# A two-layer graph network on one core: how the second layer contracts the scalars of x with the aggregate, and where its one-hots are made

## The chip, the cores and the metric

The kernel runs on one core of a Trainium2 chip. The metric is the device time of one execution in microseconds (us); before the change it is 6655.41 us, the median of three runs (6651.92 to 6660.94).

## The reference, cut to what matters

There are 12500 nodes with 160 features each (64 scalars, 32 vectors of three components) and 200000 edges. Two layers run one after the other; each builds a message per edge, sums the messages by destination node into an aggregate of the same form as x, and updates each node with bilinear products of x and the aggregate, before a layer norm.

```python
agg = segment_sum(msg, row)                 # 12500 x 160
a0, a1 = agg[:, :64], agg[:, 64:].reshape(n, 32, 3)
u0 = einsum('nu,nv,uvw->nw', xs, a0, Wu_ss) * INV64 \
   + einsum('nui,nvi,uvw->nw', xv, a1, Wu_vv) * (INV_SQRT3 * INV32)
u1 = einsum('nu,nvi,uvw->nwi', xs, a1, Wu_sv) * c + einsum('nui,nv,uvw->nwi', xv, a0, Wu_vs) * c
u0 = u0 + xs @ Lu_s * INV8
u1 = u1 + einsum('nui,uw->nwi', xv, Lu_v) * INV_SQRT32
x = layernorm(x + node_features + concat([u0, u1]))
```

The change is about the first term of `u0` in the second layer, the scalar product of xs (64) and a0 (64) with the 64x64x64 tensor `Wu_ss`.

## The kernel before, in words

The nodes are cut into NT = 100 tiles of HM = 125 nodes. The edges were sorted by an early stage into 2176 slots per tile (17 blocks of 128, padded), and the messages of a layer are written into those slots in DRAM. A layer's node sweep then goes over the tiles. In layer 1 (the second; layers are numbered 0 and 1 in the code) only this sweep runs, in `node_sweep`, which takes NT + 2 steps and is written out in full for every step. The five engines each have their own program of the sweep, `node_step`, and meet at semaphores only. In step t:

- SyncE (SP) issues the transfers: tile t of x (`xt`, L569, after the h of tile t - 2), the messages of tile t + 1 (`msgs`, L384) and its spilled sums once the edges of tile t - 1 are summed, and the output of tile t - 2 (L404, L405) when it is normed.
- TensorE (PE) does `bilinear(0)` to `bilinear(5)` of tile t - 1, `sum_edges` of tile t (L1368: 17 blocks of one-hot times messages into `node_ps`), the transposes of the vector products `turn_q`, `scalar_sums`, `turn_y`, `vector_products` and `linear`.
- VectorE (DVE) does `scalars(0..3)` (L1043), the mixed products (L1079, two of three components), their sums (`mixed_sum`, L1092) and `h` (L1122) of tile t - 1, in that order, and a reciprocal (L1127) of tile t - 2 between the two sums.
- ScalarE (ACT) copies the mixed products out of PSUM (`prods_out`, L1606), does the statistics of tile t - 2, the copies of x, of the aggregate and of the transposes, and at the end of the step the 17 squared distances (`distances`, L1714) and the selection (`selections`, L1720) that make the one-hots of tile t + 1 in the only buffer, `onehot`.
- GpSimd (POOL) does the third component of the mixed products of tile t - 1 (L763), and the outer products of vectors (`q3`, L737) with their two sums (L772) of tile t, once both `turn_q` of tile t - 1 have read `q3`.

The scalar product is made in two contractions. `bilinear(r)`, r = 0 to 3, multiplies the weights with the transposed aggregate (contraction over 64 on each half of the array) into a pair of PSUM banks of 1000 columns. DVE multiplies them with the transposed scalars of x into `zs` (L1043). `scalar_sums` adds them over 128 partitions with a band of ones, 32 matmuls of 32 output rows (L1325):

```python
for r in range(R0):
    for hh in range(2):
        o = BAND - row_sum(r, hh)
        for q in range(QUARTER):
            mm = te.matmul(to[32 * q:32 * q + 32, 0:HM], band[:, o:o + 32], zs[:, r, hh, q, :], ...
```

`bilinear(r)` for r of 2 and more waits until DVE has used the banks of r - 2. Layer 0 has the same products, between its own work for the edges of layer 1; it keeps them.

## Time and profile before

| what | value |
|---|---|
| median of three runs | 6655.41 us (6651.92 to 6660.94) |
| the profiled execution, its own time | 6649.59 us |
| its span in the profile | 6647.9 us |
| mean granted TensorE clock | 0.918 of full speed |
| busy: PE, DVE, ACT, POOL | 82%, 82%, 56%, 77% of the span |
| the sweep of layer 1 | from about 4850 us to the end |

The profile names each group of instructions by its source line, engine and the tensors it writes and reads ("out<-in"). "x" is the number of instructions, "busy" the time in which they ran. "Idle before" is time that the engine stood still ahead of them, with the instruction that released it. L1306 and L1307 are the matmuls of `bilinear(0..3)`, L1309 and L1310 those of `bilinear(4)` and `bilinear(5)`, L1336 those of `vector_products`. The timeline gives the start and the duration of merged pieces. A float32 matmul appears as two instructions.

### The profile page before, as it was taken

How to read it: one execution, taken by the hardware profiler on the slowest of the kernel's cores; microseconds unless marked ns; L12 is line 12 of the kernel's file. 1: busy time of each engine (PE TensorE's matmuls, PEld its weight loads, DVE VectorE, ACT ScalarE, POOL GpSimd, SP SyncE). 2: the span in 40 equal slices, each digit the busy share in tenths (PEclk: the TensorE clock that was granted, in tenths of full speed). 3: DMA queues.
4: the chain of work that ended last, by engine and by line, in shares of the span. 5: the costliest groups of instructions: out<-in, count | busy, mean ns of one | idle time of the engine just before them, and what ended most of it. 6: DMA issues, size and time to landing. Idle time of an engine off the chain costs nothing.

```text
span 6647.9 us, 144690 instructions
## 1 busy us (share of the span) xinstructions
PE 5431.9 (82%) x52095; PEld 4342.4 (65%) x52095; DVE 5458.2 (82%) x7292; ACT 3710.3 (56%) x11578; POOL 5133.5 (77%) x4006
## 2 busy tenths in 40 slices
PE   5566666666666499999999999999589999999998
PEld 3445444554545377777777777777467777777777
DVE  6777777777778589999999999989378888888988
ACT  2333333333333366666666666666267777777776
POOL 2777777777777568888888888877778888888887
PEclk7778888778788799999999999999799999999999
DMA  7888888888886278888888888888422232222222
GB/s 226 257 256 260 256 257 256 258 253 258 260 257 204 92 236 275 278 272 272 275 275 273 272 278 265 271 264 269 153 88 94 95 103 94 94 96 102 94 95 76
DMA packets 681145, 1380.94 MB, mean 208 GB/s; under 512 B 106047, under 2 KB 487661, under 8 KB 654447
## 3 DMA queue, kind: packets, MB, share of 16 engines
q1 hardware_dynamic: 527695, 1090.23, 52.2%
q0 software_dynamic: 152736, 281.45, 12.5%
q8 instruction: 416, 6.82, 0.4%
q14 instruction: 298, 2.44, 0.1%
HBM read 587.20 MB, written 784.08 MB: 206 GB/s over the span
## 4 chain that ended last, share of the span: by engine, by line
PE 36%; SPq 14%; DVE 13%; POOL 13%; DMA 9%; ACT 8%; issue 6%; POOLq 0%; DVEq 0%; ACTq 0%
PE node_ps L1368 11%; PE prods_ps L1306 6%; DMA rec<-edge_recs 5%; DVE upd L1092 5%; ACT onehot L1714 5%; POOL q L737 4%; PE prods_ps L1325 4%; SPq L353 4%; POOL q L772 3%; SPq L379 3%; PE s_ps L1222 3%; DMA table<-tab 2%; DVE zs L1043 2%; POOL picks_sb L763 2%; PE prods_ps L1309 2%
## 5 line engine op out<-in xcount | busy, mean ns | idle before, releaser
L654 POOL DMA_INDIRECT slots<-pay,slot_all x3136 | 3246.8, 1035 | 1037.0 <-issue 813.1
L1714 ACT ACTIVATE onehot<-node_iota,msgs 128x125 f32<-128x125 f32 x3400 | 1028.1, 390 | 121.9 <-POOLq L698 121.9
L1368 PEld LDWEIGHTS node_ps<-msgs,onehot 128*125 128x125 f32 x6800 | 932.0, 188 | 139.4 <-ACT onehot L1720 83.1
L1368 PE MATMUL node_ps<-msgs,onehot 128*125 128x160 f32 x6800 | 980.8, 303 | 35.9 <-ACT onehot L1720 25.3
L1092 DVE TENSOR_REDUCE upd<-work 125x48 f32<-125x3072 f32 x300 | 1004.1, 3347 | 6.8
L1079 DVE TENSOR_TENSOR work<-prods_ps,yv 125x1024 f32<-125x1024 f32 x800 | 931.3, 1217 | 52.0 <-PE prods_ps L1310 51.1
L737 POOL TENSOR_TENSOR q<-xt,yv 125x3072 f32<-125x3072 f32 x100 | 547.7, 5477 | 302.1 <-PE turn_ps L1355 285.1
L1500 ACT COPY picks_sb<-s_ps 125x512 f32<-125x512 f32 x392 | 229.9, 586 | 938.6 <-PE s_ps L1204 706.3
L1190 PE MATMUL prods_ps<-bucket_onehot,after_bf 128*128 128x500 bf16 x392 | 174.9, 446 | 667.5 <-DVE bucket_onehot L909 666.9
L1222 PE MATMUL m_ps<-win,picks_sb 125*128 125x160 f32 x3136 | 654.2, 336 | 68.6 <-ACT pay L1515 61.7
L1222 PEld LDWEIGHTS m_ps<-win,picks_sb 125*128 125x128 f32 x3136 | 519.4, 215 | 145.6 <-ACT pay L1515 91.2
L1190 PEld LDWEIGHTS prods_ps<-bucket_onehot,after_bf 128*128 128x128 bf16 x392 | 40.3, 103 | 715.4 <-DVE bucket_onehot L909 714.2
L1043 DVE TENSOR_TENSOR zs<-prods_ps,x_t 128x1000 f32<-128x1000 f32 x400 | 460.6, 1192 | 55.9 <-PE prods_ps L1307 55.9
L1306 PE MATMUL prods_ps<-spill_tab,w_bil 64*128 64x125 f32 x3200 | 439.9, 281 | 58.0 <-DVE zs L1043 58.0
L772 POOL TENSOR_TENSOR q<-q 125x1024 f32<-125x1024 f32 x200 | 473.0, 2365 | 15.7
L1043 DVE TENSOR_TENSOR zs<-prods_ps,spill_tab 128x1000 f32<-128x1000 f32 x400 | 460.4, 1192 | 10.9 <-PE prods_ps L1307 10.8
L1306 PE MATMUL prods_ps<-a_t,w_bil 64*128 64x125 f32 x3200 | 440.6, 281 | 29.9 <-DVE zs L1043 28.2
L1307 PE MATMUL prods_ps<-a_t,w_bil 64*128 64x125 f32 x3200 | 457.9, 285 | 0.0
L1307 PE MATMUL prods_ps<-spill_tab,w_bil 64*128 64x125 f32 x3200 | 457.3, 284 | 0.0
L1515 ACT COPY pay<-m_ps 128x320 f32<-128x320 f32 x784 | 331.0, 422 | 222.2 <-PE m_ps L1222 221.1
L1306 PEld LDWEIGHTS prods_ps<-spill_tab,w_bil 64*128 64x128 f32 x3200 | 385.7, 187 | 98.1 <-DVE zs L1043 76.1
L1720 ACT ACTIVATE onehot<-onehot,ones_f 128x1375 f32<-128x1375 f32 (+2 forms) x300 | 444.3, 1481 | 3.4
(268 smaller groups left out, 13339.8 us busy)
## 6 DMA issues: line engine op xcount, KB each, us to landing
msgs<-slots SPq DMA_DIRECT2D x200, 1428.0 KB, 6.4
slots<-zero SPq DMA_DIRECT2D x183, 1386.0 KB
win<-table SPq DMA_DIRECT2D x784, 160.0 KB
picks<-picks_sb SPq DMA_DIRECT2D x196, 512.0 KB
picks_sb<-picks SPq DMA_DIRECT2D x196, 512.0 KB
table<-tab SPq DMA_DIRECT2D x200, 350.0 KB
slots<-pay,slot_all POOLq DMA_INDIRECT x3136
spill_in<-spill_sums SPq DMA_DIRECT2D x200, 80.0 KB, 6.1
```

Of the source, the lines that this page charges most:

```text
L654: g.indirect_dma_start(out=slots[layer][:, :], out_offset=bass.IndirectOffsetOnAxis(ap=slot_all[:, j:j + 1], axis=0), in_=pay[q][:, j - UB ...
L737: g.tensor_tensor(q3[0:HM, VV * i0:].rearrange("p (i u v) -> p i u v", u=V, v=V), xt[nb][0:HM, S:D].rearrange("p (u i) -> p i u", i=3)[:, ...
L772: add = g.tensor_tensor(q3[0:HM, 0:VV], q3[0:HM, 0:VV], q3[0:HM, VV * (j + 1):VV * (j + 2)], ALU.add)
L1043: ve.tensor_tensor(zs[:, r, :, :, :], prods_ps[(nb + r) % 2][:, :].rearrange("p (h c) -> p h c", h=2)[:, :, 0:QUARTER * HM].rearrange("p h ...
L1079: ve.tensor_tensor(wk[:, i, :, :].rearrange("p w (h k) -> p h w k", h=2), prods_ps[(nb + r) % 2][0:HM, :].rearrange("p (h w k) -> p h w k" ...
L1092: ve.tensor_reduce(upd1[:, :, w0:w0 + ROUND // KV], mixed_part(r), AX_X, ALU.add).then_inc(s["upd"], 1)
L1222: mm = te.matmul(to[:, D * j:D * j + D], (pick_b[q] if layer else pick_n[hh])[0:WROWS, P * (2 * p + j):P * (2 * p + j) + P], win[q][0:WROW ...
L1306: te.matmul(to[:, HM * q:HM * q + HM], w.bil[0:S, o:o + P], a2_t[nb][0:S, :], start=True, stop=True)
L1307: mm = te.matmul(to[:, 512 + HM * q:512 + HM * q + HM], w.bil[S:P, o:o + P], a2_t[nb][S:P, :], start=True, stop=True)
L1368: te.matmul(node_ps[0:HM, 0:D], onehot[:, j, :], msgs[b][:, j, 0:D], start=(j == 0), stop=False)
L1714: last = ac.activation(onehot[:, j, :], node_iota[:, :], ACT.Square, bias=msgs[b][:, j, LOCAL:LOCAL + 1], scale=-1.0)
L1720: return ac.activation(onehot[:, j0:j1, :], onehot[:, j0:j1, :], ACT.Relu, bias=ones_f[:, 0:1], scale=-2.0)
```

## The change

The scalar product of layer 1 is made in one contraction. Let a be the transposed scalars of the aggregate, which `turn_y` leaves in `s_ps[:, 2 * HM:3 * HM]`, v on the partitions, twice. For each pair of indices (u, v) the product x[u] * a[v] is formed first, and then contracted with `Wu_ss` over the 4096 pairs, 128 at a time.

- The transposed scalars of x come from layer 0: `ts_t` (64 x 125), which its `table_turn` makes anyway, is also stored to DRAM (`x0_t`, one 32 KB transfer per tile), and ACT waits for that store before it writes `ts_t` again.
- In layer 1 SP spreads them (`spread_x`): for each of four parts z, two transfers of 8 rows (1000 floats in one run) of `x0_t` to 64 partitions each, all 64 the same. Three parts have two buffers (in `zs`, and in `pay`, `picks_sb`, which layer 1's sweep leaves free); the fourth has one, and its transfer is issued behind the messages.
- DVE multiplies each part in place with `s_ps` (`spread_scaled`, 128 x 1000), in place of `scalars(r)`.
- PE contracts each part with 8 matmuls, 64 output rows on either half of the columns, straight into `node_ps` (`scalar_products`), in place of `bilinear(0..3)` and `scalar_sums`. `vector_products` goes on in the same bank, and `linear` adds both halves with `folded`.
- `bilinear(4)` and `bilinear(5)` have a pair of banks each, and wait for the use of the same pair by the tile before.
- The one-hots of odd tiles go to a second place (`win` and `tab`), in runs of 5, 5, 5 and 2 blocks. ACT makes the distances of tile t + 1 in two parts of 9 and 8 blocks, ahead of and behind `summed` and the first `turned_q`; the selection (`chosen`) is behind `scalars_out`; the statistics of tile t - 2 come behind the second part; `features` is right behind `prods_out`.
- Messages and spilled sums are loaded two tiles ahead, after the edges of the tile itself. Some semaphores of the layers are joined.

```diff
 (SP, layer 1)
+                if layer == 1 and within(t, 0, NT):
+                    for z in range(SPREAD - 1):
+                        spread_x(k, z)
+                if layer == 1 and within(t, 0, NT - 2):
+                    sp.wait_ge(s["edges_done"], t + 1)
+                    load_msgs(layer, later(later(k)))
+                    load_spilled(layer, later(later(k)))
+                if layer == 1 and within(t, 0, NT):
+                    spread_x(k, SPREAD - 1)
...
                 if layer == 0 and within(t, 2, NT + 2):
                     store_table(1, (t - 2, half - 1, b))
+                    sp.dma_start(x0_t[t - 2], ts_t[:, :]).then_inc(LS[1]["x_put"], 16)
+
+            def spread_x(k, z):
...
+                behind = 2 if z < SPREAD - 1 else 1
+                if within(t, behind, NT):
+                    sp.wait_ge(s["scaled_used"], SPREAD * (t - behind) + z + 1)
+                for hh in range(2):
+                    frm = x0_t[t, S // 2 * hh + PER * z:S // 2 * hh + PER * (z + 1), :].rearrange("u n -> (u n)")
+                    sp.dma_start(xs[b][z][S * hh:S * hh + S, :, :].rearrange("p r n -> p (r n)"), frm.unsqueeze(0).broadcast_to([S, PER * HM])
+                                 ).then_inc(s["xs_in"][b] if z < SPREAD - 1 else s["xs_last"], 16)
 (DVE)
+                def spread_scaled(z):
+
+                    ve.wait_ge(s["y_turned_out"], 3 * n + 3)
...
+                    ve.tensor_tensor(xs[nb][z][:, :, :], xs[nb][z][:, :, :], s_ps[:, 2 * HM:3 * HM].unsqueeze(1).broadcast_to([P, PER, HM]),
+                                     ALU.mult).then_inc(s["scaled"], 1)
...
-                    for r in range(R0):
-                        scalars(r)
+                    for z in range(SPREAD):
+                        spread_scaled(z)
 (PE)
+                def scalar_products():
...
+                    te.wait_ge(s["y_out"], Y_OUT * min(t + 1, NT))
+                    for z in range(SPREAD):
+                        te.wait_ge(s["scaled"], SPREAD * n + z + 1)
+                        for r in range(PER):
+                            o, half_of = S * (PER * z + r), S * (r % 2)
+                            mm = te.matmul(node_ps[half_of:half_of + S, 0:HM], w.bil[:, o:o + S], xs[nb][z][:, r, :],
+                                           start=(z == 0 and r < 2), stop=False, tile_position=(0, half_of))
+                        mm.then_inc(s["scaled_used"], 1)
...
                 if layer == 1:
-                    for r in range(SUMS):
+                    for r in range(R0, SUMS):
                         bilinear(r)
                     sum_edges()
                     turn_q(0)
-                    scalar_sums()
+                    scalar_products()
                     turn_q(1)
 (ACT)
                 if layer == 1:
                     prods_out(0)
                     prods_out(1)
+                    features()
+                    if within(t, 0, NT - 1):
+                        distances(1, later(k), 0, HOT_HALF)
+                    summed()
+                    turned_q(0)
+                    if within(t, 0, NT - 1):
+                        distances(1, later(k), HOT_HALF, BLOCKS)
                     if within(t, 2, NT + 2):
                         deviation(layer, t - 2)
-                    features()
-                    summed()
-                    turned_q(0)
                     turned_q(1)
                     turned_y()
                     scalars_out()
+                    if within(t, 0, NT - 1):
+                        chosen(later(k))
                     normal()
-                    if within(t, 0, NT - 1):
-                        one_hot(later(k))
                     return
```

What the change moves is seen best in the order of the instructions. On PE, in a step of layer 1 before (the matmuls of `bilinear(5)`, then `sum_edges`, `turn_q(0)`, `scalar_sums`, `turn_q(1)`; ahead of them stand 32 rows of `bilinear(0..3)`):

```order
L1309 MATMUL prods_ps<-w_bil,spill_tab 125x512 [waits prods_used_l1]
L1310 MATMUL prods_ps<-w_bil,spill_tab 125x512
L1368 MATMUL node_ps<-msgs,onehot 125x160 [waits y_out_l1,spill_in0_l1,hot_l1]
L1368 MATMUL node_ps<-msgs,onehot 125x160 x16
L1369 MATMUL node_ps<-spill_in,ident 125x160
L1355 MATMUL turn_ps<-ident,q 128x125 [waits q_part_l1]
L1355 MATMUL turn_ps<-ident,q 128x125 x3
L1325 MATMUL prods_ps<-zs,band 32x125 [waits copied_l1,prods_used_l1]
L1325 MATMUL prods_ps<-zs,band 32x125 x31
L1355 MATMUL turn_ps<-ident,q 128x125 [waits q_turned_out_l1]
```

and now, from `sum_edges` on (L1435), with the four parts of `scalar_products` at L1391:

```order
L1435 MATMUL node_ps<-msgs,onehot 125x160 [waits y_out_l1,spill_in0,hot_l1]
L1435 MATMUL node_ps<-msgs,onehot 125x160 x16
L1436 MATMUL node_ps<-spill_in,ident 125x160
L1422 MATMUL turn_ps<-ident,q 128x125 [waits q_part_l1]
L1422 MATMUL turn_ps<-ident,q 128x125 x3
L1391 MATMUL node_ps<-pay,w_bil 64x125 [waits scaled_l1,y_out_l1]
L1391 MATMUL node_ps<-pay,w_bil 64x125 x7
...
L1391 MATMUL node_ps<-zs,w_bil 64x125 [waits scaled_l1]
L1391 MATMUL node_ps<-zs,w_bil 64x125 x7
L1422 MATMUL turn_ps<-ident,q 128x125 [waits q_turned_out_l1]
```

The wait for DVE's products stood ahead of `sum_edges` and stands behind it now; the second `turn_q` stays behind the contraction.

On ACT, one step of layer 1 now, from `features` to `normal` (`turned_y` at L1711 to L1713 is left out):

```order
L1667 COPY xa<-xt 125x128 [waits q_mul_l1,prods_used_l1,mixed_mul_l1,y_turned_l1,x_in0_l1]
...
L1790 ACTIVATE win<-node_iota,msgs 128x125 x8
L1693 COPY xa<-node_ps 125x128 [waits edges_done_l1]
L1694 COPY yv<-node_ps 125x3x32
L1686 COPY q_t<-turn_ps 128x500 [waits out0_l1,q_turned_l1]
L1790 ACTIVATE win<-node_iota,msgs 128x125 [waits edges_done_l1,msgs_in1_l1]
...
L1622 ACTIVATE sq,stats<-h 125x160 [waits normed_l1,h_ready_l1]
...
L1721 COPY spill_tab<-node_ps 128x125 [waits lin_l1,out0_l1]
...
L1638 ACTIVATE res<-centred,stats 125x160 [waits stored0_l1,inverse_l1]
```

The copy of x now stands ahead of nine distances and of the copy of the aggregate, and the statistics stand behind them.

On SP's queue, one step of layer 1 now:

```order
L592 DMA xt<-x_mid 128x160 [waits q_mul_l1,h_ready_l1]
L629 DMA zs<-x_t 64x1000 [waits scaled_used_l1]
L629 DMA zs<-x_t 64x1000
...
L407 DMA msgs<-slots 128x2856 [waits edges_done_l1]
L634 DMA spill_in<-spill_sums 128x160
...
L427 DMA out<-res 112x160 [waits normed_l1]
L428 DMA out<-res 13x160
```

Before, `xt`, `msgs`, `spill_in` and the two parts of `out` were all; eight transfers L629 are new, six ahead of `msgs` and two ahead of `out`.

## Rows read from the trace of the kernel before

**Rows 1.** Windows: start:end, length, busy per engine (instructions), PEclk, DMA share, GB/s.
```profile
core 0: us, PE busy (x) PEld busy (x) DVE busy (x) ACT busy (x) POOL busy (x), PEclk, DMA share, GB/s
0.00:1400.00 1400.00, 868.41 (x4619) 663.02 (x4619) 1013.23 (x2694) 457.27 (x1419) 986.39 (x986) 0.79 0.83 253
2200.00:4700.00 2500.00, 2347.88 (x24054) 1876.71 (x24054) 2235.01 (x1793) 1612.22 (x5510) 1957.73 (x1823) 0.99 0.80 259
4800.00:6600.00 1800.00, 1632.11 (x20033) 1345.23 (x20034) 1577.09 (x1198) 1338.47 (x3734) 1467.99 (x502) 0.99 0.29 97
```

**Rows 2.** Instructions on tile q in layer 1: POOL's outer product, first and last start.
```profile
L737 POOL TENSOR_TENSOR q<-xt,yv x97: 5470/5477/5485, 4848.4 to 6567.8; 125x3072 f32<-125x3072 f32 x97
```

**Rows 3.** The chain that ended last, two steps of layer 1: start, us, what.
```profile
5796.92 5.49 POOL q L737
...
5802.48 2.37 POOL q L772
5804.93 2.18 POOL q L772
...
5807.24 2.39 POOL picks_sb L763
5809.63 2.13 POOL work L763
5811.76 3.26 DVE upd L1092
...
5824.65 4.81 PE node_ps L1368 x34
...
5832.76 5.49 POOL q L737
```

**Rows 4.** Timeline of one step of layer 1: start, us, engine, instruction, idle before.
```profile
5804.85 0.18 PEld L1309 LDWEIGHTS prods_ps<-w_bil,spill_tab 64*125 64x125 f32 x1 [0.39 <-DVE zs L1043]
...
5807.14 2.36 DVE L1079 TENSOR_TENSOR picks_sb<-prods_ps,yv 125x1024 f32<-125x1024 f32 x2 [1.23 <-PE prods_ps L1310]
5811.68 3.34 DVE L1092 TENSOR_REDUCE upd<-picks_sb 125x48 f32<-125x3072 f32 x1
5812.53 1.92 PE L1325 MATMUL prods_ps<-zs,band 128*32 128x125 f32 x64
...
5814.38 0.65 PE L1355 MATMUL turn_ps<-ident,q 125*128 125x125 f32 x4
...
5815.69 1.08 PE L1336 MATMUL prods_ps<-q_t,w_vv 128*64 128x125 f32 x16 [0.34 <-ACT q_t L1614]
...
5817.30 5.03 ACT L1714 ACTIVATE onehot<-node_iota,msgs 128x125 f32<-128x125 f32 x17
...
5817.49 0.37 PE L1306 MATMUL prods_ps<-a_t,w_bil 64*128 64x125 f32 x1
```

**Rows 5.** Timeline of VectorE around the step's end.
```profile
5818.71 2.30 DVE L1043 TENSOR_TENSOR zs<-prods_ps,x_t 128x1000 f32<-128x1000 f32 x2
```

**Rows 6.** Groups of layer 1 (4850 to 6580 us): busy, mean ns, idle before.
```profile
L1720 ACT ACTIVATE onehot<-onehot,ones_f 128x2125 f32<-128x2125 f32 x97 | 200.7, 2069 | 3.1
L1606 ACT COPY pay<-prods_ps 125x1024 f32<-125x1024 f32 x194 | 189.1, 1003 | 3.8 <-PE prods_ps L1310 0.2
```

**Rows 7.** Transfers in 5000 to 6500 us: by queue, and by issue (KB, us to landing).
```profile
q1 hardware_dynamic: 48980, 142.11, 27.8%
...
msgs<-slots SPq DMA_DIRECT2D x83, 1428.0 KB, 6.4
xt<-x_mid SPq DMA_DIRECT2D x83, 80.0 KB, 1.9
```

**Rows 8.** Loads of the weights to 64 partitions each: the issues, and two windows there.
```profile
L441 SPq DMA_DIRECT2D w_bil<-u_ss x4: 576/612/616, 191.4 to 220.6; - x4
...
198.00:202.00 4.00, 0.00 (x0) 0.00 (x0) 3.76 (x9) 0.00 (x0) 3.07 (x3) 0.71 1.09 247
202.00:206.00 4.00, 0.20 (x1) 0.23 (x2) 1.25 (x8) 0.59 (x1) 2.88 (x3) 0.50 1.08 401
```

More of the change, by code:

```diff
@@ L47 @@
 HOT = (0, 4, 11, BLOCKS)
+HOT_HALF = 9
 LAG = 7
@@ L68, with used @@
 DIRECT = (3, 2)
-USES = [R0 + d * R1 for d in DIRECT]
-def used(layer, r):
-    return r + 1 if r < R0 else R0 + DIRECT[layer] * (r + 1 - R0)
+USES = [R0 + DIRECT[0] * R1, DIRECT[1] * R1]
+SPREAD = 4
+PER = S // 2 // SPREAD
+def used(r):
+    return r + 1 if r < R0 else R0 + DIRECT[0] * (r + 1 - R0)
 def row_sum(r, half):
@@ L1361, in sum_edges @@
                     te.wait_ge(s["hot"], t + 1)
-                    te.wait_ge(s["spill_in"][b], 16 * half + 16)
+                    te.wait_ge(spill_in_by[b], 16 * (NT // 2 * layer + half + 1))
                     if layer == 0 and within(t, 2, NT):
@@ L1367, in sum_edges @@
                     for j in range(BLOCKS):
-                        te.matmul(node_ps[0:HM, 0:D], onehot[:, j, :], msgs[b][:, j, 0:D], start=(j == 0), stop=False)
+                        te.matmul(node_ps[0:HM, 0:D], hot_blocks[layer * b][j], msgs[b][:, j, 0:D], start=(j == 0), stop=False)
                     te.matmul(node_ps[0:HM, 0:D], idn, spill_in[b][0:HM, :], start=False, stop=True).then_inc(s["edges_done"], 1)
@@ L1373, in linear @@
                         return
-                    if layer == 0 and edges:
-                        te.wait_ge(s["y_out"], Y_OUT * t + Y_OUT)
-                    if layer == 1 and within(n, 1, NT):
+                    if layer == 0:
+                        if edges:
+                            te.wait_ge(s["y_out"], Y_OUT * t + Y_OUT)
+                    elif within(n, 1, NT):
                         te.wait_ge(s["h_ready"], n)
@@ L1381, in linear @@
                     te.wait_ge(s["ss_out"], n + 1)
-                    te.matmul(to[0:HM, 0:S], ss_t[:, :], in_order[:, :], start=False, stop=True).then_inc(s["lin"], 1)
+                    te.matmul(to[0:HM, 0:S], ss_t[:, :], (in_order, folded)[layer][:, :], start=False, stop=True).then_inc(s["lin"], 1)
                 def turn_y():
@@ L1471, in table_turned @@
                     ac.wait_ge(s["t_mm"], m)
+                    if layer == 1:
+                        ac.wait_ge(s["x_put"], 16 * m)
                 ac.copy(ts_t[:, :], turn_ps[0:S, 0:HM])
@@ L1645, in scalars_out @@
                         return
-                    ac.wait_ge(s["prods"], RS_ALL * n + RS_ALL)
+                    ac.wait_ge(s["out0"], n + 1)
                     if within(n, 1, NT):
                         ac.wait_ge(s["lin"], n)
-                    ac.copy(ss_t[:, :], prods_ps[(nb + SUMS) % 2][:, 0:HM]).then_inc(s["ss_out"], 1)
+                    ac.copy(ss_t[:, :], (prods_ps[(nb + SUMS) % 2] if layer == 0 else node_ps)[:, 0:HM]).then_inc(s["ss_out"], 1)
                 def normal():
@@ L1710, in distances @@
                 ac.wait_ge(s["msgs_in"][b], 16 * half + 16)
-                if within(t, 1, NT):
-                    ac.wait_ge(s["edges_done"], t)
+                if within(t, 1 + layer, NT):
+                    ac.wait_ge(s["edges_done"], t - layer)
                 for j in range(j0, j1):
-                    last = ac.activation(onehot[:, j, :], node_iota[:, :], ACT.Square, bias=msgs[b][:, j, LOCAL:LOCAL + 1], scale=-1.0)
+                    last = ac.activation(hot_blocks[layer * b][j], node_iota[:, :], ACT.Square, bias=msgs[b][:, j, LOCAL:LOCAL + 1], scale=-1.0)
                 last.then_inc(squared[layer], 1)
@@ L1720, in selections, with chosen @@
                 return ac.activation(onehot[:, j0:j1, :], onehot[:, j0:j1, :], ACT.Relu, bias=ones_f[:, 0:1], scale=-2.0)
-            def one_hot(k):
-                distances(1, k, 0, BLOCKS)
-                selections(1, k[0] + 1, 0, BLOCKS).then_inc(LS[1]["hot"], 1)
+            def chosen(k):
+                t, half, b = k
+                ac.wait_ge(squared[1], 2 * t + 2)
+                for run in hot_runs[b]:
+                    last = ac.activation(run, run, ACT.Relu, bias=ones_f[:, 0:1], scale=-2.0)
+                last.then_inc(LS[1]["hot"], 1)
             ac.wait_ge(placed, UNITS)
-            ac.wait_ge(LS[0]["sp_done"], 1)
+            ac.wait_ge(spills_done, 1)
             distances(0, (0, 0, 0), HOT[0], HOT[1])
@@ L1744, with laid_out @@
 }
-def laid_out(name, a):
+def laid_out(name, a, layer):
+    if name == "u_ss" and layer == 1:
+        return np.ascontiguousarray(a.transpose(1, 0, 2).reshape(S, SS))
     if name in ("u_ss", "u_vs"):
@@ L1753, in laid_out @@
         return np.ascontiguousarray(a.transpose(0, 2, 1))
-    if name == "u_vv":
+    if name == "u_vv" and layer == 0:
         places = np.arange(S)
@@ L1779 @@
     attr = given("edge_attr", np.ascontiguousarray(inputs["edge_attr_4"]).reshape(-1))
-    weights = [{k: given(f"{k}_{layer}", laid_out(k, np.asarray(inputs[names[layer]])))
+    weights = [{k: given(f"{k}_{layer}", laid_out(k, np.asarray(inputs[names[layer]]), layer))
                 for k, names in _WEIGHTS.items()} for layer in range(2)]
```

136 lines of the change are left out of this document (83 added, 53 removed).

## The prediction

> **What bounds the kernel now.** I read the windows first. The sweep of layer 0 (2200 to 4700 us) and that of layer 1 (4800 to 6600 us) are both dense on several engines [rows 1]; the change touches layer 1 and gives layer 0 one small transfer per tile. In layer 1 the transfers are light: 29% of the queues' time, 97 GB/s [rows 1]. POOL's outer product starts 97 times from 4848.4 to 6567.8 us [rows 2], so a tile costs 1719.4 / 96 = 17.91 us, and the 100 tiles have about 99 such periods. A microsecond of the period is worth 99 us.
>
> The chain of waits shows what makes up the 17.91 us [rows 3]. It takes two tiles to close: POOL's outer product at 5796.92, its two sums, its two mixed products, DVE's two sums (3.26 each), h, DVE's first products of the next tile, `bilinear(2..5)`, `sum_edges` (4.81), the transposes, and POOL again at 5832.76: 35.84 us for two periods. PE's 17 edge blocks and its `bilinear` stand in that chain behind DVE.
>
> Beside the chain, each engine has a sum of its own. DVE, from starts in the timeline: 5807.14 to 5811.68 is 4.54 us for the four mixed products; 5811.68 [rows 4] to 5818.71 [rows 5] is 7.03 us for both sums, the reciprocal and h; two products on `zs` take 2.30 us [rows 5], so four take 4.6 us, less some overlap between neighbours. Together 16.1 us of 17.91. DVE is close to full, and no change of the other engines can go below that. ACT has 1338.47 / 1800 x 17.91 = 13.3 us of work in a period and POOL 14.6 us [rows 1].
>
> **The change part by part.** *DVE*: four `scalars` of 128 x 1000, one input in PSUM and one in SBUF, become four `spread_scaled` of 128 x 1000, again one input in PSUM and one in SBUF. No row shows this form; between nothing less and the 1024-element form at 2.36 / 2 = 1.18 us against 1.15 [rows 4, 5] I take the same 4.6 us. DVE's floor stays 16.1 us. The gain can only be what DVE waits today: 17.91 - 16.1 = 1.8 us.
>
> *PE*: the 64 instructions of `bilinear(0..3)` and their waits go, which is the stretch from 5817.49 to the next `bilinear(4)`; what stays runs from 5804.85 to 5817.49 = 12.64 us [rows 4]. In it `scalar_sums` holds 5812.53 to 5814.38 = 1.85 us and is replaced by `scalar_products`: 32 matmuls, 64 instructions, of the form of L1336 (128 x 64, 125 columns, alternate halves), of which 16 take 1.08 us [rows 4]. Bounds: 4 x 1.08 = 4.3 us, or, with the end of each part hidden under the next, 64 x 0.054 + 0.2 = 3.7 us (16 instructions less a tail of 0.2 give 0.054). The parts follow one another, so 3.7. PE then needs 12.64 - 1.85 + 3.7 = 14.5 us, less than DVE.
>
> *The chain with the new order.* The wait for DVE's products is now behind `sum_edges`, so PE does its 4.81 us of edges [rows 3] while DVE is still in its sums. What remains of the two-tile chain: POOL from 5796.92 to 5811.76 is 14.84 us [rows 3], DVE's sums and h 7.03, its four products 4.6, the last part on PE and `turn_q(1)` about 1.7 (16 instructions 1.08, transposes 0.65) [rows 4]: 28.2 us for two tiles, 14.1 a tile. That chain no longer binds.
>
> *ACT and SP*, the price of the new order. `features` of tile t waits for `xt`, which SP issues only after h of tile t - 2 and behind the output of tile t - 3, and that output waits for `normal`, ACT's last act in step t - 1. That is a loop: ACT from `features` to `normal`, then SP's issues, then the landing. ACT's part: 13.3 us less two copies of 1.0 [rows 6], which fit into the rest of the loop, = 11.3; the selection of odd tiles in four runs instead of one adds a fixed part each, between 0 and 3 x 0.4, I take 0.6, half of it on average: 0.3; waits for PE inside (`vector_products` 1.08 before the copy of `ss_t`, and its start) 0.7 to 1.8, I take 1.3; SP's queue 1.0 for three issues, landing 1.9 of `xt` [rows 7], semaphores 0.3. Sum 16.1 us. It is as long as DVE's floor.
>
> *Transfers*. New per tile: 2 x 64 x 4000 B x 4 = 2.05 MB. Old: 142.11 MB at a 27.8% share in 1500 us with 83.8 tiles is 5.0 us of all 16 engines per tile [rows 7]. The nearest rows for the spread loads are those of the weights, also 64 partitions at a time: there the engines were full (1.09) at 247 GB/s, and 401 GB/s in the window after [rows 8]. At 247 GB/s the spread takes 8.3 us, and 13.3 us with the rest, under 16.1. It also fits in time: six parts go out when h is done, the last two behind `msgs`; DVE needs them only three products (3.5 us) into the next step. The Trainium skill, page SBUF — State Buffer, section "Door 1: The DMA port swizzle", says that bandwidth depends on how many of 16 ports the partitions reach, and that partitions 0 to 63 reach one port of each pair, so a transfer to 64 partitions has half of about 436 GB/s, 218. By that the spread takes 9.4 us and the transfers 14.4; the sum would be the same, with less room. Rows 8 agree in direction.
>
> *Layer 0*: one store of 32 KB per tile and one more issue on SP. If its 24.7 us steps were bound by transfers it would cost 32 KB / 259 GB/s = 0.13 us a tile [rows 1], 13 us; if not, nothing. DMA share is 0.80 and PE is at 94% there, so I take 3 us. The messages loaded two tiles ahead and the two one-hot buffers cost nothing: their 6.4 us [rows 7] are under a whole step.
>
> *Sum*. Floor 16.1 by two loops that are equally long and meet at h and at the reciprocal; two such loops do not run at the floor of each, so I take 16.5 us for the period: (16.5 - 17.91) x 99 = -140, +3 for layer 0. The profiled execution took 6649.6 us, so 6512.6; the median of the runs is 5.8 us above it, and the forecast against it is **6518 us**.
>
> **The rivals.**
> 1. *ACT and SP bind* (a new wait in place of the old). `xt` is now in the same queue behind up to 0.5 MB of spread rows; if it lands 2 us late, or ACT's waits are at their upper bound, the loop is 16.1 + 1 to 1.5 = about 17.2: (17.2 - 17.91) x 99 = -70, 6588 us. For it: the loop's sum has no slack. Against: the last part is issued long before h. Chance 0.17.
> 2. *The spread loads bind* (the slower side). 64 partitions read the same 4000 bytes at a time, and no row shows a load whose source repeats. The transfers become the period when 2.05 MB take over 17.91 - 5.0 = 12.9 us, at under 159 GB/s. At half the rate of rows 8, 124 GB/s, they take 16.5 + 5.0 = 21.5 us: +3.6 x 99 = +356, 7011 us. Against it: 4000 bytes in one run is a good length, and `msgs` with long runs reaches 1428 KB in 6.4 us. Chance 0.13.
> 3. *The clock falls.* From 0 to 1400 us PE was busy 62% and was granted 0.79; at 91% it was granted 0.99 [rows 1]. PE will be busy 14.5 of 16.5 us, 88%. At 0.8 it would need 14.5 / 0.8 = 18.1 us, about today's time or 20 us more, 6675. Chance 0.03.
> 4. *Nothing changes*: a wait of DVE on ACT's copy (1.23 us on the mixed products today [rows 4]) stays, since ACT has not less to do. Then the period stays near 17.9, 6655 us. Against: ACT's 5.03 us of distances [rows 4] and 2.07 of selection [rows 6], behind which that copy queues today, are cut into parts under `sum_edges`. Chance 0.05.
>
> **How the numbers follow.** The forecast has 0.62. Its own range runs from DVE's floor everywhere, (16.1 - 17.91) x 99 = -179, 6476, to 16.9 a tile, 6560. The range of 8 in 10 adds the first rival up to 17.8 a tile, 6645: 6476 to 6645 holds 0.79, with about 0.16 above and some beyond rival 1. A measurement of this kernel can tell 0.2%, 13 us, from no change. Faster by more than that: forecast and rival 1, 0.79. Within it: rival 4, 0.05. Slower: rivals 2 and 3, 0.16.
>
> **What the profile of the changed kernel would show.** DVE busy over 95% in layer 1, its idle time ahead of the mixed products gone, POOL's outer products 16.5 us apart, the chain mostly on DVE in every tile; transfers at about 3.7 MB / 16.5 us = 225 GB/s with a share of 0.8; PE with waits in front of the parts of `scalar_products`. Wrong would be: DVE idle in front of its products behind a transfer of `zs` or `pay` (rival 2), ACT idle in front of the copy of `xt` and DVE idle behind ACT (rival 1), PEclk under 0.95 (rival 3), four products on DVE that take over 1.2 us each (a floor above 16.1).

## The result, and the profile after

| | before | after |
|---|---|---|
| median (lowest to highest) | 6658.16 us (6651.92 to 6660.94, 4 runs) | 6490.56 us (6482.34 to 6497.87, 4 runs) |
| ratio to before | | 0.975, 95% interval 0.9738 to 0.9762 |
| the profiled execution | 6649.59 us | 6484.03 us |
| its mean granted clock | 0.918 | 0.913 |
| period of layer 1's sweep | 17.91 us | 16.22 us |

The forecast was 6518 us, with a range of 6476 to 6645. The period is read as before from POOL's outer product, now at L777. This row answers to [rows 2]:

```profile
L777 POOL TENSOR_TENSOR q<-xt,yv x100: 5468/5479/5487, 4851.0 to 6456.8; 125x3072 f32<-125x3072 f32 x100
```

(6456.8 - 4851.0) / 99 = 16.22 us. Before, all hundred of them ran from 4848.4 to 6621.6 us, (6621.6 - 4848.4) / 99 = 17.91. So the sweep is 99 x 1.69 = 167.4 us shorter, it begins 2.6 us later, and what follows the last outer product takes 0.8 us less: -165.6 us together, the difference of the two profiled executions.

The windows of after, layer 0 and layer 1, with the columns of [rows 1]:

```profile
2200.00:4700.00 2500.00, 2345.87 (x24054) 1875.15 (x24054) 2232.37 (x1792) 1611.23 (x5510) 1958.51 (x1822) 0.99 0.80 260
4800.00:6400.00 1600.00, 1373.81 (x13475) 1144.44 (x13476) 1524.47 (x1169) 1306.52 (x3796) 1435.36 (x491) 0.97 0.82 230
```

Layer 0 is as before. In layer 1 DVE went from 88% to 1524.47 / 1600 = 95%, POOL from 82% to 90%, ACT from 74% to 82%, while PE fell from 91% to 86%: it has less work, 1373.81 / 1600 x 16.22 = 13.9 us a tile after 1632.11 / 1800 x 17.91 = 16.2. The transfers went from 97 to 230 GB/s and the DMA share from 0.29 to 0.82. The granted clock fell a little, from 0.99 to 0.97.

DVE's timeline after, one tile (start, us, engine, instruction):

```profile
5866.08 4.50 DVE L1096 TENSOR_TENSOR zs<-zs,s_ps 128x1000 f32<-128x1000 f32 x4
...
5870.51 2.35 DVE L1133 TENSOR_TENSOR picks_sb<-prods_ps,yv 125x1024 f32<-125x1024 f32 x2
...
5875.03 3.34 DVE L1146 TENSOR_REDUCE upd<-picks_sb 125x48 f32<-125x3072 f32 x1
...
5882.07 2.29 DVE L1096 TENSOR_TENSOR pay<-pay,s_ps 128x1000 f32<-128x1000 f32 x2
```

The differences of the starts are 4.43 us for the four new products, 4.52 for the mixed ones and 7.04 for the sums, the reciprocal and h: 15.99 us with no idle time, and the 1.23 us that stood before the mixed products in [rows 4] are gone. Between neighbouring h of the sweep (4850 to 6450 us, 97 distances) the distance is 15.9 to 16.05 us in 68 and longer in 29, up to 18.37; the mean is 16.21. So the kernel runs at DVE's floor in 70% of its tiles, and what the mean has above it, 0.22 us, comes from the rest. One of the 29, by h's own rows, is 5817.23 - 5798.90 = 18.33 us:

```profile
5798.90 0.33 DVE L1176 TENSOR_TENSOR h<-m_ps,upd 125x160 f32<-125x160 f32 x1 [0.57 <-PE m_ps L1450]
...
5809.28 3.35 DVE L1146 TENSOR_REDUCE upd<-picks_sb 125x48 f32<-125x3072 f32 x1 [1.11 <-issue]
...
5813.64 0.16 DVE L1181 RECIPROCAL stats<-stats 125x1 f32<-125x1 f32 x1 [1.00 <-ACT stats L1628]
...
5817.23 0.33 DVE L1176 TENSOR_TENSOR h<-m_ps,upd 125x160 f32<-125x160 f32 x1
```

What ACT, POOL and PE do in this long tile, from the timeline of all engines:

```profile
5805.58 0.30 ACT L1667 COPY xa<-xt 125x128 f32<-125x128 f32 x1 [2.56 <-DMA xt<-x_mid]
...
5806.82 2.37 POOL L803 TENSOR_TENSOR picks_sb<-pay,yv 125x1024 f32<-125x1024 f32 x1
...
5809.29 3.64 PE L1391 MATMUL node_ps<-zs,w_bil 128*64 128x125 f32 x64 [1.71 <-ACT yv L1694]
```

ACT was held by `xt` for 2.56 us, and PE by ACT's copy of the aggregate for 1.71 us. DVE's own two waits are named by other rows: the 1.11 us ahead of its first sum ended 0.09 us after POOL's mixed product on `picks_sb` (5806.82 + 2.37 = 5809.19), although the profile gives "issue" for it, and the 1.00 us ahead of its reciprocal ended with ACT's statistics. So it is in the sweep (4880 to 6440 us): DVE waits 11 times ahead of the first sum, 10.2 us in all, 10 of them just behind that product of POOL, and 9 times for the statistics, 4.2 us in all. The waits of the sweep (4850 to 6400 us): engine, line, what it waited for, us in total, times, longest:

```profile
ACT xa L1667 <- DMA xt<-x_mid: 152.5, 96, 3.3
POOL q L777 <- PE turn_ps L1422: 111.4, 95, 4.5
...
PEld node_ps L1391 <- ACT yv L1694: 72.1, 84, 2.7
...
DVE zs L1096 <- DMA zs<-x_t: 3.7, 2, 3.3
```

ACT waits for `xt` in every tile, 152.5 / 96 = 1.59 us, and DVE waits for a spread part twice in the whole sweep. Who holds `xt` back is told by the chain that ended last (start, us, what; the same long tile and the start of the next) and by the waits of SP's own queue (5000 to 6400 us):

```profile
5801.63 0.41 SPq L428
5802.13 3.43 DMA xt<-x_mid
...
5809.71 2.33 ACT onehot L1790 x8
...
5815.45 1.72 ACT onehot L1803
...
5817.42 0.42 ACT res L1638
...
5818.25 1.52 SPq L428
5819.87 1.81 DMA xt<-x_mid
```

```profile
SPq L427 <- ACT res L1638: 353.2, 87, 4.6
SPq L592 <- DVE h L1176: 7.9, 17, 1.0
```

This is the loop that the prediction priced: `features`, distances, selection, `normal`, the output's two issues, `xt`, `features`. It goes through ACT's `res` and the output in most tiles; h (DVE) came last in 17 of 87. In this tile a landing of 3.43 us made it longer than DVE's sum. Over the tiles the length of the period goes with the time from h to ACT's copy of x (correlation 0.81 over 94 tiles). Over the sweep (4850 to 6400 us) ACT has 34.5% of the chain, PE and POOL 16% each, the transfers and DVE 10.7% and 10.6%; DVE had 25.8% before. The prediction expected this chain to be mostly on DVE; it is not. So two loops of nearly equal length run side by side: DVE's, which is constant, and this one, which scatters.

### The profile page after: what moved, and what is told of

Read it like the earlier page. It is cut to its first block, busy times and chain, and to the rows that moved or that the text cites. A ratio compares the mean times of both kernels' runs of the same rounds, so it can differ in the third digit from the quotient of the medians.

```text
span 6482.3 us, 133337 instructions
## 1 busy us (share of the span) xinstructions
PE 5231.3 (81%) x45695; PEld 4209.8 (65%) x45695; DVE 5447.3 (84%) x7293; ACT 3699.9 (57%) x11728; POOL 5135.4 (79%) x4006
## 4 chain that ended last, share of the span: by engine, by line
PE 34%; ACT 17%; DMA 14%; POOL 12%; issue 9%; DVE 7%; SPq 6%; POOLq 0%; ACTq 0%; DVEq 0%
POOL slots L694 8%; PE node_ps L1435 7%; ACT onehot L1790 7%; DMA slots<-pay,slot_all 6%; PE prods_ps L1362 5%; PE s_ps L1276 3%; PE node_ps L1391 3%; POOL q L777 3%; DMA xt<-x_mid 3%; PE prods_ps L1379 3%; PE m_ps L1276 2%; DMA rec<-edge_recs 2%; ACT win L1790 2%; POOL q L812 2%; PE prods_ps L1403 2%
## 5 line engine op out<-in xcount | busy, mean ns | idle before, releaser
L1790 ACT ACTIVATE onehot<-node_iota,msgs 128x125 f32<-128x125 f32 x2550 | 783.0, 392 | 122.2 <-POOLq L738 122.2
L1435 PEld LDWEIGHTS node_ps<-msgs,onehot 128*125 128x125 f32 x5100 | 701.7, 189 | 101.3 <-ACT onehot L1796 40.1
L1435 PE MATMUL node_ps<-msgs,onehot 128*125 128x160 f32 x5100 | 738.2, 303 | 35.9 <-ACT onehot L1796 14.2
L777 POOL TENSOR_TENSOR q<-xt,yv 125x3072 f32<-125x3072 f32 x100 | 548.0, 5480 | 133.7 <-PE turn_ps L1422 116.2
L751 POOL TENSOR_TENSOR q<-xt,yv 125x512 f32<-125x512 f32 x300 | 323.0, 1079 | 102.7 <-PE turn_ps L1422 79.1
L1422 PE MATMUL turn_ps<-ident,q 125*128 125x125 f32 x1600 | 258.9, 284 | 120.1 <-POOL q L812 95.3
L1146 DVE TENSOR_REDUCE upd<-picks_sb 125x48 f32<-125x3072 f32 x100 | 334.3, 3343 | 10.4 <-issue 6.7
L1276 PE MATMUL node_ps<-win,picks_sb 125*128 125x160 f32 x1568 | 341.0, 347 | 2.5 <-ACT pay L1587 2.5
L1258 PE MATMUL s_ps<-ident,picks_sb 128*125 128x128 f32 x1568 | 324.3, 341 | 20.2 <-ACT picks_sb L1572 16.7
L1276 PE MATMUL s_ps<-win,picks_sb 125*128 125x160 f32 x1568 | 322.1, 329 | 0.0
L1096 DVE TENSOR_TENSOR zs<-zs,s_ps 128x1000 f32<-128x1000 f32 x250 | 284.6, 1187 | 25.9 <-ACT v_t L1713 22.0
## 6 DMA issues: line engine op xcount, KB each, us to landing
msgs<-slots SPq DMA_DIRECT2D x200, 1428.0 KB, 10.4
```

The source lines that it names most:

```text
L751: g.tensor_tensor(q3[0:HM, VV * i + V * u0:VV * i + V * u0 + VV // 2].rearrange("p (u v) -> p u v", v=V), xt[nb][0:HM, S:D].rearrange("p ( ...
L777: g.tensor_tensor(q3[0:HM, VV * i0:].rearrange("p (i u v) -> p i u v", u=V, v=V), xt[nb][0:HM, S:D].rearrange("p (u i) -> p i u", i=3)[:, ...
L1146: ve.tensor_reduce(upd1[:, :, w0:w0 + ROUND // KV], mixed_part(r), AX_X, ALU.add).then_inc(s["upd"], 1)
L1258: mm = te.transpose(s_ps[0:WROWS, P * j:P * j + P], pick_e[hh][:, UB // 2 * part + j, :, :].rearrange("p n c -> p (n c)"), ident[:, :])
L1276: mm = te.matmul(to[:, D * j:D * j + D], (pick_b[q] if layer else pick_n[hh])[0:WROWS, P * (2 * p + j):P * (2 * p + j) + P], win[q][0:WROW ...
L1435: te.matmul(node_ps[0:HM, 0:D], hot_blocks[layer * b][j], msgs[b][:, j, 0:D], start=(j == 0), stop=False)
```

## The experiments

Each kernel was run beside the kernel before on the same chip. The period is (last start - first start) / 99 of POOL's outer product.

| run | median us (runs) | ratio to before, 95% | period us |
|---|---|---|---|
| e1, contraction with the old order of ACT | 7037.57 (4) | 1.0571 [1.0554, 1.0589] | 21.83 |
| e2, one-hots alone | 6984.39 (4) | 1.0492 [1.0474, 1.0509] | 21.21 |
| e8, one-hots alone, early statistics | 6708.33 (4) | 1.0076 [1.0059, 1.0093] | 18.46 |
| e3, `xt` ahead | 6469.76 (4) | 0.9718 [0.9701, 0.9735] | 15.97 |
| e4, 7/8 of a product out | 6482.33 (4) | 0.9731 [0.9714, 0.9747] | 16.19 |
| e5, both | 6425.10 (4) | 0.9654 [0.9638, 0.9670] | 15.57 |
| e6, spread in one transfer | 6468.77 (2) | 0.9715 [0.9696, 0.9735] | 16.05 |
| e7, own rows as source | 6481.65 (2) | 0.9735 [0.9715, 0.9754] | 16.18 |
| e9, the change again | 6486.23 (5) | 0.9736 [0.9721, 0.9750] | 16.16 |
| e10, e3 again | 6475.91 (5) | 0.9720 [0.9707, 0.9733] | 15.95 |

### One half at a time

**e1.** The change with the old places of the one-hots and the statistics on ACT.

```diff
                     prods_out(1)
+                    if within(t, 2, NT + 2):
+                        deviation(layer, t - 2)
                     features()
-                        distances(1, later(k), 0, HOT_HALF)
                     summed()
                     turned_q(0)
-                        distances(1, later(k), HOT_HALF, BLOCKS)
-                        deviation(layer, t - 2)
                     turned_q(1)
                     turned_y()
                     scalars_out()
+                    normal()
+                        distances(1, later(k), 0, HOT_HALF)
+                        distances(1, later(k), HOT_HALF, BLOCKS)
                         chosen(later(k))
-                    normal()
```

> The changed kernel with ScalarE's old order in layer 1 (statistics, features, summed, transposes, normal, then all 17 distances and the selection); everything else of the change stays. If the new contraction is the whole gain and the order of the one-hots is only decoration, 6490 us (16.2 us a tile). If my account holds, normal waits for DVE's reciprocal some 12.6 us into the step, 7.3 us of one-hots come behind it, and sum_edges with all that follows on PE starts about 4 us later: about 17.3 us a tile, +110, 6600 us, with PE waiting for onehot or win.

Measured: 7037.57 us, 380 us above before. The expectation missed by far. The chain of one tile of this run, gap free but for short pieces:

```profile
5805.09 3.64 PE node_ps L1391 x64
...
5809.98 1.10 PE node_ps L1403 x16
...
5811.26 0.27 ACT res L1638
...
5811.59 4.44 ACT win L1788 x15
...
5817.37 1.51 ACT win L1801 x2
...
5819.32 6.67 PE node_ps L1435 x34
...
5826.46 0.25 ACT yv L1694
```

From the `yv` ahead of the first row (5804.80) to the last row 21.66 us, and everything in it belongs to PE or ACT, one after the other: the contraction, the vector products, the output, the distances, the selection, the edges. Before the change, `bilinear(0..3)` kept PE busy while ACT made the one-hots. The contraction that replaces it stands behind the edges, so nothing is left to cover them. On top of that the edges take 6.67 us here where the same 34 instructions took 4.81 in [rows 3]. The windows of 2 us show why:

```profile
5816.00:5818.00 2.00, 0.00 (x0) 0.00 (x0) 0.63 (x1) 1.97 (x5) 1.92 (x2) 0.54 1.03 240
5818.00:5820.00 2.00, 0.68 (x2) 0.68 (x3) 0.00 (x0) 2.00 (x4) 1.82 (x1) 0.50 1.04 238
5820.00:5822.00 2.00, 2.00 (x9) 2.00 (x9) 1.75 (x2) 1.94 (x6) 1.76 (x1) 0.50 0.24 54
```

PE stood still from about 5813.8 to 5819.3; the granted clock fell to 0.50, which is the 1.2 GHz level, while it did, and stayed there until 5822, well into the edges. Over the sweep (4900 to 6900 us) it was 0.86 on average. Of the 5.61 us by which this period is longer than after's, the clock accounts for about 6.67 - 4.81 = 1.9 in a tile like this one, and the series of ACT and PE for the rest; the two were not run apart.

**e2.** The kernel before with the other half: second place for the one-hots, loads two tiles ahead, ACT's new order. The scalar product stays in two contractions.

```diff
 (SP, layer 1)
-                    load_spilled(layer, later(k))
+                if layer == 1 and within(t, 0, NT - 2):
+                    sp.wait_ge(s["edges_done"], t + 1)
+                    load_msgs(layer, later(later(k)))
+                    load_spilled(layer, later(later(k)))
 (PE, sum_edges)
-                        te.matmul(node_ps[0:HM, 0:D], onehot[:, j, :], msgs[b][:, j, 0:D], start=(j == 0), stop=False)
+                        te.matmul(node_ps[0:HM, 0:D], hot_blocks[layer * b][j], msgs[b][:, j, 0:D], start=(j == 0), stop=False)
 (ACT)
-                    if within(t, 2, NT + 2):
-                        deviation(layer, t - 2)
                     features()
+                        distances(1, later(k), 0, HOT_HALF)
                     summed()
                     turned_q(0)
+                        distances(1, later(k), HOT_HALF, BLOCKS)
+                        deviation(layer, t - 2)
...
-                    normal()
-                        one_hot(later(k))
+                        chosen(later(k))
+                    normal()
```

> The kernel before with only the one-hot half of the change (second set, distances in two parts, messages two tiles ahead, features early); the scalar product stays in two contractions. My account: DVE no longer waits for ACT's copy, but PE's own work of about 17.5 us a tile and the coupling with DVE stay, 17.6 us a tile, 6625 us. The rival, that the one-hots give half of the gain by themselves, 6570 us.

Measured: 6984.39 us, 326 above before: again a miss by far. The statistics of tile t - 2 come late on ACT, and DVE's reciprocal, ahead of its second sum, waits for them. They also stand ahead of the second copy of `q_t`, for which PE's `vector_products` waits. Both, from the waits in 4900 to 6600 us:

```profile
PEld prods_ps L1339 <- ACT q_t L1617: 201.9, 80, 2.5
...
DVE stats L1130 <- ACT stats L1559: 178.1, 80, 2.4
```

That is 2.2 us a tile on DVE, which here is in the two-tile chain of [rows 3], and 2.5 us on PE. PE's own rows in two neighbouring tiles:

```profile
5810.12 1.08 PE L1339 MATMUL prods_ps<-q_t,w_vv 128*64 128x125 f32 x16 [2.27 <-ACT q_t L1617]
```

```profile
5829.94 1.93 PE L1339 MATMUL prods_ps<-q_t,w_vv 128*64 128x125 f32 x16 [2.27 <-ACT q_t L1617]
```

After the same wait the same 16 instructions take 1.08 us in one tile and 1.93 in the next. The window behind the second wait:

```profile
5830.00:5832.00 2.00, 2.00 (x17) 1.68 (x18) 2.00 (x1) 0.45 (x4) 2.00 (x1) 0.50 0.04 11
```

**e8.** To see how much of e2 is the statistics, they go back to their old place, and nothing else is changed in e2.

```diff
                     prods_out(1)
+                    if within(t, 2, NT + 2):
+                        deviation(layer, t - 2)
                     features()
...
-                    if within(t, 2, NT + 2):
-                        deviation(layer, t - 2)
                     turned_q(1)
```

> As the second experiment (one-hot half alone), with the statistics back in front of features. If DVE's 2.1 us wait for the reciprocal, and PE's stretches at half clock that follow from it, are what the half alone costs, the granted clock returns to 0.99 and the time to 17.6 us a tile, 6630. If the early one-hots themselves upset the order, it stays above 6900.

Measured: 6708.33 us; 276 of e2's 326 us are gone, (6984.39 - 6708.33), and the clock is back, as the window of the sweep shows:

```profile
4900.00:6900.00 2000.00, 1615.88 (x19969) 1331.03 (x19967) 1575.21 (x1172) 1317.60 (x3827) 1448.76 (x487) 1.00 0.24 83
```

The place of four short statistics on ACT was worth 2.75 us a tile there, wait and clock together. The time is 78 us above the 6630 that was expected, and 49 above the kernel before. The chain of this run goes from POOL through ACT's distances and its copies of `yv` and `q_t` to `vector_products`, `linear` and `bilinear(0)`:

```profile
5824.30 1.87 ACT onehot L1721 x7
...
5827.67 1.34 ACT onehot L1721 x5
...
5830.00 0.47 ACT q_t L1617
5830.51 1.07 PE prods_ps L1339 x16
```

While PE's products stand ahead of the edges, the copies behind distances hold PE up; that reading rests on the chain, and no run took it apart. So the one-hots in parts are no gain by themselves. They cost 0.76%, and pay only together with the contraction that moves behind the edges. The change with the statistics in their old place was not run.

### What binds now

**e3.** `xt` is loaded a tile ahead, behind the last spread part, and no longer waits for the output and h.

```diff
-                if within(t, 0, NT):
+                if layer == 0 and within(t, 0, NT):
...
+                if layer == 1 and t == 0:
+                    load_x(k)
+                    load_x(later(k))
...
+                if layer == 1 and within(t, 1, NT - 1):
+                    sp.wait_ge(s["q_mul"], t)
+                    load_x(later(k))
```

> The changed kernel with xt of tile t + 1 issued ahead of the output in step t, after q_mul of tile t - 1, without a wait for h. If the loop ScalarE - SP - transfer binds (16.22 us a tile against DVE's 16.0), ACT's 1.6 us of waiting for xt goes and the period falls to DVE's floor: -20 us, 6470. If DVE alone binds, nothing changes: 6490 within 6 us.

**e4.** DVE has less to do: of the fourth product only the first of 8 rows is multiplied.

```diff
+                    if z == SPREAD - 1:
+                        ve.tensor_tensor(xs[nb][z][:, 0:1, :], xs[nb][z][:, 0:1, :], s_ps[:, 2 * HM:3 * HM].unsqueeze(1).broadcast_to([P, 1, HM]),
+                                         ALU.mult).then_inc(s["scaled"], 1)
+                        return
```

> The changed kernel with seven eighths of DVE's fourth spread_scaled left out (0.9 us less of DVE per tile; the other rows are used without the factor). If DVE binds, -0.85 x 99 = -84 us, 6406. If the loop of ScalarE, SP and xt binds, no change, 6490; if both are equally long, a little, 6480.

Measured: e3 6469.76 us with a period of 15.97, e4 6482.33 us with 16.19. The windows of the sweep, of e3 first and then of e4:

```profile
4800.00:6400.00 1600.00, 1380.53 (x13599) 1150.05 (x13600) 1532.92 (x1177) 1321.34 (x3834) 1453.92 (x502) 0.97 0.84 232
```

```profile
4800.00:6400.00 1600.00, 1369.32 (x13446) 1140.11 (x13446) 1444.94 (x1166) 1304.39 (x3792) 1435.75 (x495) 0.97 0.82 230
```

With DVE freed (e4, busy 90%) the mean stays at 16.2. Its tiles are no longer alike: between neighbouring h there are 15.4 us at the shortest tenth and 17.2 at the longest, and only 13 of 97 lie at 15.9 to 16.05. In this run DVE waits ahead of its first sum 92 times (4880 to 6440 us), 70 us in all, and in 91 of them POOL's product on `picks_sb` had ended 0.09 us before. So DVE now follows POOL, whose own loop of 15.4 us (see e5) is the length of e4's short tiles; what makes the mean 16.2 is the loop of ACT, SP and `xt`, since opening it as well (e5) takes 16.19 - 15.57 = 0.62 us away. With that loop opened (e3, DVE busy 96%) 93 of 98 distances lie at 15.9 to 16.05 and 5 above, where the change has 29 of 97. So DVE sets the floor of the change, and the 0.2 us above it go when this loop is opened.

**e5.** Both edits together; what comes next must show.

> xt ahead as in the third experiment, and seven eighths of DVE's fourth product left out as in the fourth. If the two loops are the only ones near 16 us, the period falls to the next engine's floor, POOL's 5.48 + 4.8 + 4.7 = 15.1 and a wait for turn_q, or DVE's 15.1: about 15.3 us a tile, 6400 us. If a third loop stands at 16 us too, 6470.

Measured: 6425.10 us, period 15.57 (expected 6400). The chain of this run, from one outer product of POOL to the next:

```profile
5796.93 5.49 POOL q L789
...
5802.48 2.38 POOL q L824
...
5807.36 0.65 PE turn_ps L1438 x4
5808.00 3.57 PE node_ps L1407 x64
5811.57 0.59 PE turn_ps L1438 x4
...
5812.32 5.48 POOL q L789
```

A third loop of 5812.32 - 5796.93 = 15.39 us: POOL must not write `q3` again before the second `turn_q`, and PE makes all of `scalar_products` between the two. It is why the microsecond taken from DVE brings only 0.4 beyond e3. (POOL's wait for `turn_ps`, 111.4 us in the change, is the same place.) The prediction had no sum for this loop.

### The transfers

**e6.** The spread goes to all 128 partitions in one transfer of the same rows, so half as many issues with twice the bytes each.

```diff
-                for hh in range(2):
-                    frm = x0_t[t, S // 2 * hh + PER * z:S // 2 * hh + PER * (z + 1), :].rearrange("u n -> (u n)")
-                    sp.dma_start(xs[b][z][S * hh:S * hh + S, :, :].rearrange("p r n -> p (r n)"), frm.unsqueeze(0).broadcast_to([S, PER * HM])
+                frm = x0_t[t, PER * z:PER * (z + 1), :].rearrange("u n -> (u n)")
+                sp.dma_start(xs[b][z][:, :, :].rearrange("p r n -> p (r n)"), frm.unsqueeze(0).broadcast_to([P, PER * HM])
```

> Each part of the spread x in one transfer to all 128 partitions (both halves get the first half's rows; same bytes, half as many issues). If 64 partitions take half of the ports, the queues' share falls from 82.5% to about 68% (8.4 to 6.0 us a tile); if the repeated source sets the rate, it stays near 82%. The time: 6490 by either, at most 10 us less, since transfers do not bind.

**e7.** Each of the 64 partitions reads 4000 bytes of its own instead of the same.

```diff
-                    frm = x0_t[t, S // 2 * hh + PER * z:S // 2 * hh + PER * (z + 1), :].rearrange("u n -> (u n)")
+                    o = (8 * (t % 50) + 2 * z + hh) * S * PER * HM
+                    frm = slots[0].rearrange("r c -> (r c)")[o:o + S * PER * HM].rearrange("(p f) -> p f", p=S)
```

> The spread transfers keep their 64 partitions and their bytes but read 64 different rows of 4000 bytes (from the message slots), not one row 64 times; the values are others. If the repeated source costs, the share of the queues falls below 82.5% and landing gets shorter than 5.4 us; if the partitions set the rate, both stay. The time stays at 6490.

Queue 1 in 5000 to 6400 us (packets, MB, share of 16 engines), of after, then e6, then e7:

```profile
q1 hardware_dynamic: 105941, 323.67, 82.5%
```

```profile
q1 hardware_dynamic: 101310, 328.01, 64.7%
```

```profile
q1 hardware_dynamic: 105985, 325.31, 83.8%
```

In the change the transfers take 0.825 x 16.22 = 13.4 us of all engines a tile, of which 5.0 are the old ones [rows 7]: the spread takes 8.4 us. Taking off the same 5.0 in e6 would give 0.647 x 16.05 - 5.0 = 5.4 us, but the old transfers got shorter there too. The spread is told apart by its packets of 4000 bytes, which nothing else uses in 5000 to 6400 us. One takes 260 ns on average in the change, 187 in e6 and 267 in e7. With the 512 packets of a tile on 16 engines that is 8.3 us (246 GB/s) in the change and 6.0 us (343 GB/s) in e6, which is what the expectation had; the packets of the messages, 11424 bytes each, went from 504 to 433 ns. With sources of their own (e7) nothing gets better: the repeated source costs nothing. e6 has both all 128 partitions in one transfer and half as many transfers; which of the two does it was not run apart. The Trainium skill, page SBUF — State Buffer, section "Door 1: The DMA port swizzle", has 218 GB/s for partitions 0 to 63 and twice that for all; the runs agree in direction (e6) with a step of 260 / 187 = 1.39, from 246 GB/s, and where they differ the measured rates stand.

e6 was expected to bring 10 us at most and brought 6468.77, 17 to 22 us under the change's two medians, but from two runs; of the 22.8 us between the profiled runs, 8 lie ahead of layer 1's sweep, where the edit changes nothing. `xt` lands in 1.9 us and `msgs` in 8.1, against 2.2 and 10.4 in the change, and `out`'s second issue on SP (L428) never takes more than 771 ns, against up to 1541 in the change (423 before). With both, the loop of ACT, SP and `xt` is long in fewer tiles: 12 distances of h above 16.05 us where the change has 29. Which of the two, the landing or the issue, does it was not tried apart.

### The best version once more

**e9** is the change and **e10** is e3, five runs each on one chip.

> The changed kernel as it is, for a comparison on one chip with the next run. All accounts: 6490 us within 6.

> The kernel of the third experiment again. If the loop through SP is worth 0.25 us a tile, 20 to 25 us under the run before it, with the intervals of their ratios apart; if the 21 us between the two earlier runs was the chip's scatter, within 8 us of it.

Measured: 6486.23 (6466.68 to 6489.77) and 6475.91 us (6464.52 to 6477.31). `xt` ahead is faster twice, by 21 us against the first median of the change and by 10 us here. Here, on one chip, the two intervals of the ratio overlap, where the expectation had them apart. It is the fastest version that leaves nothing out; how much it adds, between about 0.16 and 0.32%, is not settled. The periods, 15.95 and 15.97 against 16.16 and 16.22, would give 21 and 25 us; the profiled runs' own times differ by 13 and 12, the rest being lost ahead of and behind the sweep, whose first outer product starts anywhere from 4843 to 4865 us in the profiled runs that share the change's layer 0.

## Why the prediction was right

**The two-tile chain stops binding, and DVE's sum is the floor.** Right. The forecast had 16.1 us for DVE; the measured floor is 15.99, and e3 stays at it. The four new products take 4.43 us from start to start where 4.6 was taken. One sign that was foretold is missing: the chain that ended last is not mostly on DVE (10.6% of the sweep), since the other loops are as long.

**PE's part.** `scalar_products` takes 3.64 us; 3.7 was predicted from the spacing of [rows 4]. PE has waits in front of it, as foreseen, but on ACT's `yv` (72.1 us in all), not on DVE's products.

**The loop of ACT, SP and `xt`.** Predicted at 16.1 and as long as DVE's. e4, where DVE is shortened, has a mean of 16.19 over tiles between 15.1 and 18.7; the short ones are at POOL's loop, so this loop's own length is shown only as near 16.2. The separate terms were less good than the sum: `xt` lands in 2.2 us and not 1.9, SP's issues are sometimes stretched to 1.5 us, and ACT's wait for `xt` is in every tile, long or not. Rival 1, in which this loop reaches 17.2, did not happen: `xt` isn't queued behind the last spread part, since that is issued long before.

**The transfers.** Predicted 13.3 us a tile, measured 13.4. Rival 2 (the repeated source halves the rate) did not happen, and e7 shows that the source costs nothing. By the page's 218 GB/s it would have been 14.4. That 247 GB/s was so near to 246 is in part luck: the window that it was read from [rows 8] moved 0.99 MB, of which under half (0.47 MB) went in packets of 4096 bytes and a fifth in packets of 256, so it was no clean price for loads to 64 partitions.

**Layer 0.** +3 us predicted; the sweep of layer 1 began 2.6 us later in the one pair of profiled runs. That is luck, as the same start lies between 4843 and 4865 us in the other runs with the change's layer 0: no run settles a price of this size.

**The clock.** Rival 3 did not happen: 0.97 in the sweep at 86% busy PE. But e1 and e2 show another cause than the mean load that the rival argued from: idle stretches of some microseconds. They are in the change too, in few tiles. Windows of after, in which PE waits for POOL and for ACT's `yv`:

```profile
5788.00:5790.00 2.00, 0.65 (x4) 0.41 (x4) 2.00 (x3) 2.00 (x8) 2.00 (x2) 1.00 1.01 250
5790.00:5792.00 2.00, 1.48 (x14) 1.49 (x16) 2.00 (x3) 2.00 (x9) 2.00 (x2) 0.60 0.98 237
```

The contraction takes over 4 us in 11 of 94 tiles of the change, up to 5.3, at a mean granted clock of about 0.68. The one that starts at 5790.52 takes 5.23 us; POOL's outer product behind it starts late, and its product on `picks_sb` is what holds DVE back 18.8 us later, in the long tile shown above. So it goes each time: the distance of h behind the one with such a contraction is long in all 11, 16.16 to 18.37 us, and these 11 hold 12.7 of the 20.7 us that all distances have above the floor. But a slow contraction does not do it alone: e3 has 8 of them and only 2 long distances behind them. `xt` late, a short standstill of PE and a lower clock come together in the change, and how the 0.2 us divide between them was not run apart.

**The step that was off.** The period was taken as 16.5 with the argument that two equally long loops don't run at the floor of each. That is right in kind, as the 29 long tiles show, but 0.4 us on top of 16.1 was too much: measured are 0.23 on top of 15.99. Together 0.28 us x 99 = 28 us, the whole distance of 6518 to 6490.56. That the forecast lay so near owes something to this: 16.5 was a judgement and not a sum.

**What the prediction didn't see.** It priced the change as a whole and never asked what either half is alone. Alone they cost +380 (e1) and +326 us (e2, of which 276 are the place of the statistics, so +49 in e8), together they bring -167. Adding up the prices of the halves does not give that. The contraction takes away PE's work over ACT's one-hots, and the new order of ACT takes the one-hots out of the series. The late statistics, dear in e2, cost DVE only 4.2 us of waiting in the whole sweep of the change; that this is because DVE's reciprocal is no longer in a chain that binds PE is argued, not shown.

## What to carry to other kernels

When a change moves work on one engine past work of another, ask of each moved piece what it had covered, and write down the loops (who waits for whom, once around) for the new order: here loops of 16.2, 16.0 and 15.4 us decided, and the first two, summed from the old trace, were right to about 0.1 us. Two edits of which each makes the kernel 5% slower can make it 2.5% faster together, so a half that fails alone is not refuted. The same bytes in two loads of 64 partitions took the queues 1.39 times as long as in one to all 128; here, at a DMA share of 0.82, that was worth 17 to 22 us at most.

## What was unexpected of the hardware

- In an otherwise dense sweep, PE's standing still for about 5.5 us a tile (e1) brought the granted clock to 0.50 while it stood, and the work after it ran at that level at first: the edges took 6.67 us instead of 4.81. In e2 the same wait of PE was followed by 0.50 in one tile and by 1.00 in the tile before. Such waits cost twice, and not every time.
- A load whose 64 partitions all read the same 4000 bytes is as fast as one from rows of their own: 260 and 267 ns for a packet, shares of 82.5 and 83.8% (e7).
- SP's issue of a small transfer, 0.41 us at the median, took up to 1541 ns while the DMA share was 0.82, up to 771 at 0.65 (e6), and up to 423 at 0.29.
